# Two attention stages of a one-core graph network: projection taken a quad later, inputs transposed ahead

## The reference

```python
x = x + L0_gnn(layernorm(x), adj, ...)    # attention, 4 heads, q, k and v with bias
x = x + L0_ffn(layernorm(x), ...)         # 8 experts, top 2
x = x + L1_gnn(layernorm(x), adj, ...)    # attention, 8 heads
x = x + L1_ffn(x, ...)                    # 30 rounds of tanh, silu, layernorm, product
# inside L0_gnn, per graph and head:
attn = softmax(where(adj == 0, -1e9, q @ k.T * scale))
out  = (attn @ v, heads joined) @ Wo.T + bo
return layernorm(out) * gamma + beta      # L1_gnn returns ctx @ Wo + bo, without this layernorm
```

## Time and profile before

| | |
|---|---|
| device time, median of three runs | 3301.6 us (3297.16 to 3302.17) |
| the profiled execution | 3298.23 us |
| its span, first to last instruction | 3296.5 us |
| PE busy | 2834.6 us (86%) |
| DVE busy | 2667.8 us (81%) |
| ACT busy | 2097.0 us (64%) |
| POOL busy | 1731.9 us (53%) |
| mean granted TensorE clock | 0.933 |

### The profile page before, as it was taken

One profiled execution on the slowest core, in us unless ns is written; L12 is line 12 of the kernel. 1 busy time (PEld: TensorE's weight loads), 2 busy tenths in 40 slices (PEclk: granted clock), 3 DMA queues, 4 the chain that ended last, 5 costly groups with the idle time before them and its releaser, 6 DMA issues. The chain is left out here.

```text
span 3296.5 us, 69090 instructions
## 1 busy us (share of the span) xinstructions
PE 2834.6 (86%) x20383; PEld 1865.6 (57%) x20383; DVE 2667.8 (81%) x7110; ACT 2097.0 (64%) x3936; POOL 1731.9 (53%) x1148
## 2 busy tenths in 40 slices
PE   4666666669999978888888848999999999999999
PEld 3444444468888855555555535555555555555556
DVE  4677777668888856666666568999999999999999
ACT  2333333334444435555555448999999999999995
POOL 2333334343333312221122147999999998888883
PEclk8787887779999989999999968999999999999999
DMA  4000000000000000000000003555555555555555
GB/s 130 14 13 13 15 14 13 0 14 0 0 0 0 0 21 14 13 12 10 13 13 13 1 3 134 201 203 193 195 205 197 193 200 205 192 194 205 198 193 174
DMA packets 132578, 281.67 MB, mean 85 GB/s; under 512 B 11760, under 2 KB 69152, under 8 KB 132512
## 3 DMA queue, kind: packets, MB, share of 16 engines
q1 hardware_dynamic: 115616, 272.44, 24.0%
q10 hardware_dynamic: 16896, 8.39, 0.9%
HBM read 270.49 MB, written 10.29 MB: 85 GB/s over the span
## 5 line engine op out<-in xcount | busy, mean ns | idle before, releaser
L1139 POOL TENSOR_TENSOR d_g<-d_g,d_rb 128x1024 f32<-128x1024 f32 x464 | 1083.9, 2370 | 127.6 <-DMA d_rb<-d_rstd_rows 112.4
L1340 PE MATMUL d_p_y<-d_g,d_w_main 128*128 128x512 f32 x1856 | 952.6, 595 | 0.0
L1354 PEld LDWEIGHTS d_p_gt<-ident,d_g 128*128 128x128 f32 x3840 | 450.7, 142 | 541.9 <-ACT d_g L1399 381.2
L1218 DVE BATCH_NORM_STATS2 d_stats<-d_p_gt 128x6 f32<-128x256 f32 x1920 | 713.1, 407 | 22.5 <-PE d_p_gt L1354 22.2
L1399 ACT ACTIVATE d_g<-d_th,d_bias 128x512 f32<-128x512 f32 x928 | 666.9, 719 | 12.1 <-DVE d_th L1211 0.9
L1211 DVE SCALAR_TENSOR_TENSOR d_th<-d_th,d_p_y 128x512 f32<-128x512 f32 x960 | 634.8, 661 | 4.1 <-ACT d_th L1395 4.1
L1395 ACT ACTIVATE d_th<-d_p_y,d_bias 128x512 f32<-128x512 f32 x928 | 625.5, 674 | 0.2 <-PE d_p_y L1340 0.2
L1354 PE MATMUL d_p_gt<-ident,d_g 128*128 128x128 f32 x3840 | 592.8, 278 | 0.1
L295 DVE TENSOR_REDUCE a_row_max<-a_p_s 128x4 f32<-128x512 f32 x384 | 238.4, 683 | 216.3 <-PE a_p_s L397 216.3
L541 ACT COPY a_prob_t<-a_p_w 128x512 f32<-128x512 f32 x288 | 170.2, 591 | 370.1 <-PE a_p_w L404 370.1
L214 POOL TENSOR_TENSOR a_rstd<-a_var,minus_half 128x4 f32<-128x4 f32 x64 | 65.3, 1020 | 612.1 <-PE a_p_s L397 570.6
(11 more groups left out here) (189 smaller groups left out, 3988.8 us busy)
## 6 DMA issues: line engine op xcount, KB each, us to landing
d_rb<-d_rstd_rows SPq DMA_DIRECT2D x464, 512.0 KB, 5.5
a_adj_in<-in_adj_dram SPq DMA_DIRECT2D x64, 256.0 KB, 2.8
out_dram<-d_out_sb ACTq DMA_DIRECT2D x32, 256.0 KB, 2.7
d_rstd_rows<-d_rstd_row SPq DMA_DIRECT2D x116, 16.0 KB, 1.4
m_w_sb<-in_L_ffn_w_dram SPq DMA_DIRECT2D x2, 512.0 KB
x_sb<-in_x_dram SPq DMA_DIRECT2D x1, 256.0 KB, 2.9
a_w_raw<-in_L_gnn_Wq_dram SPq DMA_DIRECT2D x2, 64.0 KB, 2.1
a_w_raw<-in_L_gnn_Wk_dram SPq DMA_DIRECT2D x2, 64.0 KB, 2.1
```

Of the source, the lines that this page charges most:

```text
L1139: nc.gpsimd.tensor_tensor(g[:, c, :], g[:, c, :], rb[:, buf, :], ALU.mult).then_inc(s_gs, 1)
L1218: ins = nc.vector.bn_stats(stats[:, q % 2, (j * CT + t) // 2].rearrange("p a s -> p (a s)"), p_gt[:, t * P:(t + 2) * P].rearrange("p (a c) ...
L1340: nc.tensor.matmul(p_y[:, c % 2, cols(u)], w_main[:], g[:, c, cols(u)], start=True, stop=True).then_inc(s_y, 1)
L1354: ins = nc.tensor.transpose(p_gt[:, t * P:(t + 1) * P], g[:, c, t * P:(t + 1) * P], ident[:])
```

## The change

- The projection of quad `k` is done two bodies later (`project(k - 2)`), in the first attention into `p_y`, in the second into `p_z`. Its bias comes from a matmul: `ones_bf` (128x128, bf16) times `bias_rows`, whose rows 0, 32 and 64 hold the bias as a sum of three bf16 numbers. Eight more small VectorE instructions at the start of each attention make these.
- `xn_t` has two halves, for even and odd quads.
- In the first attention the normalisation of `x` moves from VectorE (L288) to ScalarE, with an offset of minus mean times rstd that VectorE makes in one small instruction (`offset_x`). ScalarE also copies the projection out (before: VectorE's addition, L325). The statistics of `x` are taken three quads ahead instead of two.
- In the second attention the addition of the bias on GpSimd (L231) is gone. The statistics of `x` are taken three quads ahead.
- TensorE's, ScalarE's and VectorE's bodies are written out anew for each attention; banks are named at each step. `context_product` is cut in two halves around `shift_scores` where TensorE would wait for VectorE's copy of the maxima.

The core of the diff, with the bodies of the first attention and TensorE's body of the second:

```diff
@@ first attention (PARTS == 1) and shared steps
-        xn_t = sb("xn_t", [P, QUAD])
+        xn_t = sb("xn_t", [P, 2, QUAD])
...
+                link(nc.vector.tensor_copy(bias_part[:, 0], out_bias[:]))
+                link(nc.vector.tensor_tensor(bias_rest[:, 0], out_bias[:], bias_part[:, 0], ALU.subtract))
...
+                for i in range(3):
+                    link(nc.vector.tensor_copy(bias_rows[32 * i:32 * i + 1], bias_part[32 * i:32 * i + 1, i:i + 1]
...
+                def offset_x(k):
+                    dve.wait_ge(s_rstd, k + 1)
+                    nc.vector.scalar_tensor_tensor(offset[:]..., stats[:, :, :, 1], -1.0, rstd[:]...).then_inc(s_off, 1)
...
-                def project(k):
+                def project(k, bank):
                     pe.wait_ge(s_ctx, k + 1)
+                    nc.tensor.matmul(bank[:], ones_bf[:], bias_rows[:], start=True, stop=False)
                     for g in range(QG):
+                        last = nc.tensor.matmul(bank[:, graph(g)], context_t[:, graph(g)], w_o[:], start=False,
...
+                def first_body(k, par):                    # VectorE
+                        maxima(k)
+                        normalise_projection(k - 3, 0)
+                        take_maxima(k, p_w)
+                        normalise_projection(k - 3, 1)
+                        invert_sums(k - 1)
+                        normalise_context(k - 1)
+                        stats_x(k + 3)
+                        stats_projection(k - 2)
+                        offset_x(k + 3)
...
+                def first_body(k, par):                    # TensorE
+                        scores(k, par, 0)
+                        transpose_prob(k - 1, 2, p_w)
+                        transpose_prob(k - 1, 3, p_z)
+                        product_q(k + 1, 1 - par, p_x)
+                        pe.wait_ge(s_ptc, 4 * k)
+                        sum_prob(0)
+                        transpose_x(k + 2, p_z)
+                        transpose_maxima(k, p_w)
+                        context_product(1 - par, 0, (0, 1))
+                        shift_scores(k)
+                        context_product(1 - par, 0, (2, 3))
+                        product_k(1 - par, p_w)
+                        pe.wait_ge(s_xtc, k + 3)
+                        product_v(k + 1, 1 - par)
+                        pe.wait_ge(s_k, k + 2)
+                        transpose_prob(k, 0, p_w)
+                        pe.wait_ge(s_rden, k)
+                        project(k - 2, p_y)
+                        pe.wait_ge(s_ctx, k)
+                        transpose_prob(k, 1, p_x)
...
+                def second_body(k, par):                   # TensorE, n = 2 * k, then n = 2 * k + 1
+                        scores(k, par, 0)
+                        transpose_prob(n - 1, 2, p_w)
+                        product_v(k, par)
+                        transpose_prob(n - 1, 3, p_w)
+                        project(k - 2, p_z)
+                        transpose_maxima(n, p_w)
+                        context_product(1 - par, 1, (0, 1))
+                        shift_scores(n)
+                        context_product(1 - par, 1, (2, 3))
+                        sum_prob(1)
+                        transpose_x(k + 1, p_w)
+                        transpose_prob(n, 0, p_z)
+                        pe.wait_ge(s_xtc, k + 2)
+                        transpose_prob(n, 1, p_w)
+                        scores(k, par, 1)
+                        transpose_prob(n - 1, 2, p_z)
+                        pe.wait_ge(s_rden, k)
+                        product_q(k + 1, 1 - par, p_y)
+                        transpose_prob(n - 1, 3, p_w)
+                        product_k(1 - par, p_x)
+                        transpose_maxima(n, p_z)
+                        sum_prob(0)
+                        shift_scores(n)
+                        context_product(par, 0, range(QG))
+                        transpose_prob(n, 0, p_w)
+                        transpose_prob(n, 1, p_z)
...
+                def first_body(k, par):                    # ScalarE
+                        normalise_x(k + 2)
+                        take_prob(k - 1, 2, p_w)
+                        take_prob(k - 1, 3, p_z)
+                        take_q(k + 1, p_x)
+                        take_xn(k + 2, par, p_z)
+                        for t in range(3):
+                            exponentials(k, t)
+                        take_k(k + 1, p_w)
+                        exponentials(k, 3)
+                        take_v(k + 1, 1 - par)
+                        take_prob(k, 0, p_w)
+                        take_projection(k - 2)
+                        take_prob(k, 1, p_x)
```

More of the change, by code:

```diff
@@ L103, in graph_attention @@
         s_rstd = sem("rstd_ready")
+        s_off = sem("offset_ready")
         s_xn = sem("xn_ready")
@@ L212, in body @@
                         wait(pool, s_s, PARTS * (k + 1))
[L213 to L219, removed]
+                    if not normed:
+                        if live(k + 3):
+                            deviation_x(k + 3)
+                        if live(k + 2):
+                            edges(k + 2, par)
+                        return
@@ L362, in body @@
-                    if PARTS == 2 and live(k):
-                        maxima(PARTS * k + 1)
-                    if not normed and live(k + 2):
-                        normalise_x(k + 2)
+                    if live(k + 3):
+                        stats_x(k + 3)
+                body = first_body if PARTS == 1 else second_body
                 quads(dve, body)
+                if not normed:
+                    dve.wait_ge(s_fin, QUADS)
             @block.tensor
@@ L540, in take_prob @@
                         wait(act, s_pv, n)
-                    nc.scalar.copy(prob_t[:, t], by_graph(p_z if t == 1 else p_w)).then_inc(s_ptc, 1)
+                        wait(act, s_den, n)
+                    nc.scalar.copy(prob_t[:, t], by_graph(bank)).then_inc(s_ptc, 1)
                 def exponentials(n, t):
@@ new lines, in normalise_x, with take_xn @@
+                def normalise_x(k):
+                    act.wait_ge(s_off, k + 1)
+                    wait(act, s_xt, k)
+                    for g in range(QG):
+                        last = nc.scalar.activation(xn[:, g, :], x_sb[:, k * QG + g, :], ACT.Identity,
+                                                    bias=offset[:, g:g + 1], scale=rstd[:, g:g + 1])
+                    last.then_inc(s_xn, 1)
+                def take_xn(k, par, bank):
+                    act.wait_ge(s_xt, k + 1)
+                    wait(act, s_vmm, k - 1)
+                    wait(act, s_kmm, k - 1)
+                    nc.scalar.copy(xn_t[:, par], bank[:]).then_inc(s_xtc, 1)
@@ new lines, in second_body @@
+                def second_body(k, par):
+                    n = 2 * k
+                    if live(k - 1):
+                        take_prob(n - 1, 2, p_w)
+                    if live(k):
+                        take_v(k, par)
+                    if live(k - 1):
+                        take_prob(n - 1, 3, p_w)
+                    if live(k):
+                        for t in range(4):
+                            exponentials(n, t)
+                    if live(k + 1):
+                        take_xn(k + 1, 1 - par, p_w)
+                    if live(k):
+                        take_prob(n, 0, p_z)
+                        take_prob(n, 1, p_w)
+                        take_prob(n, 2, p_z)
+                    if live(k + 1):
+                        take_q(k + 1, p_y)
+                    if live(k):
+                        take_prob(n, 3, p_w)
+                    if live(k + 1):
+                        take_k(k + 1, p_x)
+                    if live(k):
+                        for t in range(4):
+                            exponentials(n + 1, t)
+                        take_prob(n + 1, 0, p_w)
+                        take_prob(n + 1, 1, p_z)
```

368 lines of the change are left out of this document (206 added, 162 removed).

## The result

| | before | after |
|---|---|---|
| device time, median of four runs | 3300.73 us (3297.16 to 3302.17) | 2995.34 us (2991.46 to 2996.56) |
| ratio | | 0.9074 [0.9058, 0.909] |
| profiled execution, its span | 3298.23, 3296.5 us | 2996.56, 2994.7 us |
| mean granted TensorE clock | 0.933 | 0.972 |

What follows compares the result with a forecast made beforehand. Engines waiting for each other bound the kernel, chiefly TensorE for the normalised x (first attention) and for the reciprocal (second). 3298.2 - 225 (first) - 85 (second) + 8 (ends) = 2996, stated as 2995 us; range 2960 to 3045, 80% range 2930 to 3095.

Steps and rivals of the forecast that it cites:

- The wait for the normalised x is gone: First attention: TensorE's 6.1 us wait per quad vanishes, x being normalised a body ahead; 19.57 to 12.3 us, saving 225.
- The ring ... 12.3: First attention: chain through all engines, one quad per turn; terms 11.7 us, ten handovers make 12.2, taken as 12.3.
- The signs that I named: Trace after: maxima 12.3 and 19.2 us apart, longest TensorE wait at projection for reciprocal, clock above 0.95, statistics behind ScalarE's copy.
- "19.2" in the second attention: Second attention: 17.55 us of TensorE work plus 1.65 of waits per quad, 19.2 for 21.95, saving 85 us.
- The bias at 0.24: Both attentions: the new bias matmul costs TensorE 0.24 us per quad, like one mask matmul.
- The ends, +8: Starts and drains of both attentions: small extra instructions and longer ends add 8 us, between 3 and 15.
- The clock: Both attentions: TensorE counted at full clock, from 0.80 and 0.97, as no wait over 1 us remains.
- TensorE is not the bound: Rival, both attentions: the ring is shorter than thought and TensorE's work bounds each quad; 2921 us, 12%.
- VectorE and GpSimd do not hold each other up on the ring: Rival: they still block each other, normalise_projection halves costing 2 x 1.28 in place of 0.5; 3088 us, 16%.
- The clock did not stay at 0.80 and 0.96: Rival, both attentions: many short waits keep the clock at 0.80 and 0.96; 3104 us, 7%.
- The rival by which `product_q` takes the projection's place: Rival, second attention: `product_q` waits for the reciprocal instead, the quad stays at 21.9 us; 3081 us, 3%.
- The slower one: Rival, both attentions: waits leave TensorE mostly at half speed, slower below clock 0.745; 3374 us at 0.70, 2%.

Runs made afterwards that it cites:

- experiment 5: Kernel before with 20 added 128x512 bf16 matmuls, result overwritten, in TensorE's wait for x in the first attention: 3249.24 us, 0.9848.
- experiment 3: Kernel before with only the first attention's normalisation of x moved to ScalarE, after its copy of v, with the VectorE offset: 3127.1 us, 0.9484.
- Experiment 4: Kernel after with the first attention's normalisation of x back on VectorE, at the head of its body, without the offset: 2993.07 us, 0.9073.
- Experiment 1: Kernel after with context_t in two halves, by even and odd quad: 2956.87 us, 0.8964.
- experiment 8: Kernel after without the bias matmul, the bias of both output projections left out of the result: 2985.64 us, 0.9051.
- experiment 6: Kernel before with eight added 128x512 bf16 matmuls, result overwritten, in TensorE's wait before the second attention's projection: 3276.62 us, 0.9931.
- x6_halves_ahead: Kernel after with context_t in two halves and both halves of normalise_projection ahead of VectorE's copy of the maxima: 2947.08 us, 0.8931.
- experiment 7: Kernel after with the second attention's projection one quad earlier, project(k - 1) behind the transposes of x, same bank: 3259.15 us, 0.988.
- experiment 9: The run x6_halves_ahead: kernel after, context_t in two halves, both halves of normalise_projection ahead of the maxima copy: 2947.08 us, 0.8931.
- 10: x6_halves_ahead with the first attention's normalisation of x back on VectorE, in front of the maxima: 2961.18 us, 0.8976.

## Why the prediction was right, step by step

The sum was right (301.8 us saved by the spans, 302 forecast) but in part by luck: the first attention was forecast 0.6 us a quad too short and the second 0.6 too long, some 19 us each, and these cancelled.

- **"The wait for the normalised x is gone"**: right, and the size was near (7.27 us a quad forecast, 6.65 measured). Of the 6.65 us in the first attention at least 1.6 are the clock (experiment 5) and 1.0 the rest of the order (the kernel after against experiment 3); 4.05 or less remain for the wait itself. This split is a difference of runs, and assumes that the parts add; the wait read from the rows of experiment 3, 3.9 shorter, agrees. Experiment 4 shows that in the new order ScalarE is not needed for it. In the old order the move to ScalarE, with its place, brought nearly all of it, and engine and place were not separated there.
- **"The ring ... 12.3"**: this step failed, 12.92 was measured. It listed the bank `p_y` among what waits for the reciprocal, but not the single `context_t`. VectorE's L360 waits for that very projection, and the statistics of x stand behind it. Experiment 1 puts this at 1.25 us. The forecast counted the statistics of the projection in this place. With the buffer doubled the ring is the one that I laid out, and its starts add up to 11.75. My terms without handovers came to 11.7, so they were right; what was too long were the ten handovers of 0.05 and the rounding up to 12.3. They hid half of the missing wait.
- **The signs that I named**: most came, two did not. TensorE's longest wait in a quad of the first attention was to be the projection's for the reciprocal. That one is 0.4 us; the longest is 0.9, of a group of transposes for the context, which is late by the single `context_t`. A wait for something else in each quad was my own sign of being wrong. And VectorE's statistics of the projection do not stand right behind ScalarE's copy: in the timeline above the copy ends at 212.85, and they come about 1.0 us later, behind the context and the statistics of x.
- **ScalarE's four normalisations at 1.65**: measured 1.65. A half of the projection's normalisation: 0.5 forecast, 0.59 to 0.60 measured, at the very limit that I had set.
- **"19.2" in the second attention**: 18.62 measured. The three waits were placed rightly and two were over-sized: 0.5 for `take_xn` was 0.3 and 0.7 at the maxima was 0.36, by the totals of the waits over 26 quads; the projection's wait for v was 0.6, not 0.45. Together they are 1.3 where I had 1.65. The remaining 0.2 of the error is in the work: the bias took 0.13 and not 0.24 (experiment 8), and what follows a group of transposes starts 0.43 to 0.49 behind it, where I counted nine at 0.49.
- **The bias at 0.24**: 0.21 and 0.13 (experiment 8). That GpSimd's addition of it cost nothing but at the very end is not shown by a run of its own.
- **The ends, +8**: +7.5. First maxima 2.5 later (35.5 for 33.1), the drain of the first attention 2.3 longer, the second's filling 1.5 and its drain 1.4, less 0.2 elsewhere.
- **The clock**: counted full, granted 0.99 and 1.00. Experiments 5 and 6 show that this was an effect of its own size, at least 1.6 and 0.7 us a quad (71 us in all, about a quarter of the gain). The sum contained it, as durations at full clock were used for the new order, but never said how large it was.
- **The rivals.** TensorE is not the bound in the kernel after (87% busy), but nearly so in x6_halves_ahead. VectorE and GpSimd do not hold each other up on the ring: 0.59 to 0.60 per half, where that rival had 1.28. The clock did not stay at 0.80 and 0.96. The rival by which `product_q` takes the projection's place fell, T2 did not stay. The slower one fell too, and experiment 7 shows how near its mechanism lies: one projection in the wrong place gives T2 27.2 at a clock of 0.82. Had the first attention not been better, that kernel would be slower than before. That rival was given 2%, and its condition, a clock under 0.745 in both stages, was not met even there.

## What to carry to other kernels

When a step is put later so that its engine need not wait, list every buffer that the step reads, not only the bank it writes: the one that stayed single takes back part of the gain, here 38 us for one tile. When an operation stands between a slow engine and the one that waits, ask first for a place in the order where nobody waits for it. Once it had one here, the choice of the engine paid nothing until the ring was shorter (experiments 4, 9 and 10). When TensorE waits for several us in each turn, price the wait and the clock that it costs apart; useless products put into the wait showed the second here, as a lower bound.

## What the runs showed that I had not expected

The prediction had not said that useless work can pay: twenty products more per quad made the kernel 50 us faster (experiment 5), eight more 23 us (experiment 6). The same four VectorE normalisations took 3.71 us beside GpSimd's 128x512 instructions and 1.11 us with GpSimd idle for most of them (experiment 4).

Recorded durations can change where time does not. In the recurrent layer, which is untouched, the groups of the trace for 2500 to 2800 us after (count, busy us, mean ns) show

```profile
L1400 DVE BATCH_NORM_STATS2 d_stats<-d_p_gt 128x6 f32<-128x256 f32 x450 | 229.4, 684 | 0.0
L1393 DVE SCALAR_TENSOR_TENSOR d_th<-d_th,d_p_y 128x512 f32<-128x512 f32 x226 | 212.1, 938 | 0.0
```

and before, for the same two,

```profile
L1218 DVE BATCH_NORM_STATS2 d_stats<-d_p_gt 128x6 f32<-128x256 f32 x450 | 167.0, 407 | 0.0
L1211 DVE SCALAR_TENSOR_TENSOR d_th<-d_th,d_p_y 128x512 f32<-128x512 f32 x225 | 148.7, 661 | 0.0
```

277 ns more each, with as many instructions in the same 300 us and the stage as long (1382.2 us after, 1381.7 before). Experiments 6 and 7 show the longer durations too, the others the shorter. So VectorE's busy sum of the page can't be compared between two kernels here; starts can. What makes the difference is open.
